# When the first four row gathers of a graph network kernel are released

## The reference

```
h    = layernorm(x)
m    = relu([h[src], edge_attr] @ W1.T + b1) @ W2.T + b2     # one message per edge
agg  = sum of the messages by destination                     # 10000 x 512
gi   = agg @ W_ih.T + b_ih ;  gh = h @ W_hh.T + b_hh
r, z = sigmoid(i_r + h_r), sigmoid(i_z + h_z) ;  n = tanh(i_n + r * h_n)
x1   = x + h + batchnorm((1 - z) * n + z * h)
out  = x1 + experts(layernorm(x1))                            # top 2 of 8, and a shared one
```

## Time and profile before

| what | value |
|---|---|
| median of three timed runs | 1315.35 us (1314.4 to 1319.97) |
| the profiled execution, its own time | 1303.76 us |
| its span, first to last instruction | 1301.9 us |
| PE busy | 1281.2 us (98% of the span) |
| DVE, POOL, ACT busy | 997.7, 816.4, 734.0 us |
| moved by the DMA engines | 179.58 MB, 138 GB/s on average |

### The profile page before, as it was taken

How to read it: one execution, slowest core, us unless ns; L and a number is a source line. 1 busy time by engine, 2 the same in 40 slices (tenths; PEclk the granted TensorE clock), 3 DMA queues, 4 the chain that set the end, 5 groups by cost and what they waited for, 6 DMA issues and landing times. The chain is left out here.

```text
span 1301.9 us, 22928 instructions
## 1 busy us (share of the span) xinstructions
PE 1281.2 (98%) x6398; PEld 1083.2 (83%) x6398; DVE 997.7 (77%) x2198; ACT 734.0 (56%) x1726; POOL 816.4 (63%) x1117
## 2 busy tenths in 40 slices
PE   8999999999899999999999999999999999999997
PEld 7788888888688888888888888888888888888885
DVE  6879575568777777777777777777777777777776
ACT  5331222134666666666666666666666666666652
POOL 3121243114777777777777777777778777777771
PEclk9999999999999999999999999999999999999999
DMA  8123554377433433333433433433433433433430
GB/s 297 43 83 135 198 198 162 125 273 240 141 132 130 135 122 129 137 121 129 137 121 129 136 121 129 136 122 129 137 121 129 137 121 129 137 121 129 136 98 33
DMA packets 64208, 179.58 MB, mean 138 GB/s; under 512 B 9456, under 2 KB 10352, under 8 KB 64048
## 3 DMA queue, kind: packets, MB, share of 16 engines
q1 hardware_dynamic: 48160, 99.20, 22.3%
q0 software_dynamic: 16016, 79.97, 18.6%
HBM read 141.86 MB, written 37.29 MB: 138 GB/s over the span
## 5 line engine op out<-in xcount | busy, mean ns | idle before, releaser
L1844 PE MATMUL bank<-whh_hi,x_hi 128*128 128x512 f32 x948 | 376.7, 397 | 2.4 <-DVE x L1774 1.6
L1844 PE MATMUL bank<-whh_hi,x_lo 128*128 128x512 f32 x948 | 370.1, 390 | 0.0
L1844 PE MATMUL bank<-whh_lo,x_hi 128*128 128x512 f32 x948 | 369.7, 390 | 0.0
L1844 PEld LDWEIGHTS bank<-whh_hi,x_hi 128*128 128x128 f32 x948 | 178.2, 188 | 38.6 <-DVE x L1774 2.0
L1844 PEld LDWEIGHTS bank<-whh_hi,x_lo 128*128 128x128 f32 x948 | 178.0, 188 | 37.8
L1844 PEld LDWEIGHTS bank<-whh_lo,x_hi 128*128 128x128 f32 x948 | 178.3, 188 | 34.3
L1593 POOL TENSOR_TENSOR h_n<-h,n_gate 128x512 f32<-128x512 f32 x78 | 101.0, 1294 | 68.7 <-ACT n_gate L1612 68.7
L1525 POOL TENSOR_TENSOR rstd<-var_eps,minus_half 128x1 f32<-128x1 f32 x158 | 90.4, 572 | 66.0 <-DVE var_eps L505 65.9
L1733 DVE TENSOR_TENSOR h_lo<-bank,h_hi 128x512 fp32r<-128x512 f32 x79 | 54.7, 692 | 77.8 <-ACT h_hi L1660 77.8
L1510 POOL DMA_INDIRECT gates<-gates_in,slot_at x78 | 83.7, 1074 | 46.7 <-issue 45.7
L1587 POOL TENSOR_TENSOR n_pre<-r_hn,gates 128x512 f32<-128x512 f32 x77 | 99.2, 1288 | 13.0 <-POOL r_hn L1583 13.0
(11 more groups left out here) (214 smaller groups left out, 3101.9 us busy)
## 6 DMA issues: line engine op xcount, KB each, us to landing
xt<-in_x SPq DMA_DIRECT2D x79, 256.0 KB, 2.8
x_lo_raw<-in_x_cols SPq DMA_DIRECT2D x79, 256.0 KB, 2.7
out<-y SPq DMA_DIRECT2D x78, 256.0 KB, 2.0
gates_in<-g_out SPq DMA_DIRECT2D x16, 768.0 KB, 3.9
whh_rows<-in_whh SPq DMA_DIRECT2D x4, 768.0 KB, 5.8
whh_lo_raw<-in_whh_t SPq DMA_DIRECT2D x4, 768.0 KB, 10.3
gates_in<-g_out SPq DMA_DIRECT2D x12, 256.0 KB, 4.3
wih_lo_raw<-in_wih_t SPq DMA_DIRECT2D x2, 1024.0 KB, 8.4
```

Of the source, the lines that this page charges most:

```text
L1844: last = pe.matmul(to[0:R, :], a[:, s, k * R:(k + 1) * R], w[:, k, q * D:(q + 1) * D], start=n == 0, stop=n == 3 * DK - 1)
```

## The change

The second of the two waits is gone. The four gathers are issued as soon as the source indices have landed. Nothing else in the kernel is different, neither the order of any engine's instructions nor any size.

```diff
             pool.iota(is_lo[:, :], pattern=[[0, 2]], base=0, channel_multiplier=1,
                       allow_small_or_imprecise_dtypes=True).then_inc(f2_step, 1)
-
             pool.wait_ge(src_in, 16)
-            pool.wait_ge(fused_in[DK - 1], 32)
             for j in range(SUP):
                 gather_source(0, j)
             pool.wait_ge(consts, 3)
```

## The result

Five timed runs of each kernel gave a median of 1314.63 us before (1313.3 to 1319.97) and 1320.89 us after (1319.4 to 1323.37). The ratio of after to before, taken over the runs of both, is 1.0042, with a 95% interval of 1.0026 to 1.0058 (the two medians alone lie 6.3 us apart). By the ratio the change costs about 5.5 us, between 3.4 and 7.6. That is clear of no change by its interval.

A forecast was written before the change was run, and what follows sets the result against it. PE, busy 98%, was taken to bound the kernel. Terms +0 (wait on POOL), +0 (earlier rows) and +2.4 us (third 1) on the 1315.35 us median gave 1317.8 us, range 1311.5 to 1323 us.

The forecast's parts named there:

- What bounds: Whole span: PE busy 98%; its 0.34 and 0.57 us waits at 37 to 39 us hang on third 1's landing.
- The gathers' start and worth: POOL's four gathers: first begins near 2.6 us, fourth near 7; earlier rows are worth nothing to their reader, DVE's statistics.
- The gathers' share: DMA queues from about 4.5 us: gathers get half the rate, all 1.05 MB through by 10.3 us, ahead of third 1.
- The delay of third 1, +2.4 us: Transfer of third 1: gathers' bytes delay it 2.7 us, less part of the free room, so 2.4 us.
- The 0.57 us stays: PE's second small wait at 37 to 39 us: unchanged at 0.57 us, being DVE's own work of two more tiles.
- The covers: PE before 37 us: later quarters and third 1 cause no wait; cover for third 1 is 4.7 us against 2.4.
- the case in which the clock falls: Rival on PE's clock: it falls, with the cases reaching up to 1322 us; chance 0.09.
- No measurable change: Total time: difference below 0.5%, 6.6 us, can't be told from no change by timing; chance of within 0.5%: 0.88.
- Nothing moves: Rival on the gathers: little rate while the direct queue is full, or wait never decided; 0 us, 1315.35 us; chance 0.15.
- DVE holds back the later gathers: Rival on POOL: DVE's splits hold it, only two gathers go ahead of third 1; +1.3 us, 1316.7 us; chance 0.11.
- Faster: Rival on PE's small waits: they go because something in DVE's chain comes sooner; -0.9 us, 1314.4 us; chance 0.05.
- SP's transfers: SP's eight transfers: issued some 6 to 8 us sooner, release between 11 and 13 us, no PE wait changed.

The follow-up runs named there:

- experiment 4: Kernel before, gathers still late, with SP issuing third 2 (1 MB) ahead of third 1; ratio to before 1.0026.
- experiment 7: Kernel after, with DVE's first two searches moved into later idle gaps, behind compare(0) and messages(1, 3); ratio to before 0.9983.
- experiment 1: Kernel before, unchanged, timed and profiled again; ratio to before 1.0003.
- experiment 8: Kernel before, with DVE's first two searches moved into later idle gaps, behind compare(0) and messages(1, 3); ratio to before 0.9973.
- experiment 10: Kernel before with the two searches in later gaps of DVE, plus 21 instead of 12 constant transposes on PE at the start; ratio to before 0.9978.
- experiment 2: Kernel after, with 28 transposes of a constant filling PE's gap at 37 to 41 us; ratio to before 1.0014.
- experiment 5: Kernel after, unchanged, timed and profiled again; ratio to before 1.0035.
- experiment 9: Kernel after, with SP's next eight transfers held back until third 2 has landed; ratio to before 1.0038.
- experiment 3: Kernel after, with DVE's two searches moved right behind the low parts of the four transposed tiles; ratio to before 1.0035.
- experiment 6: Kernel after, with the third and fourth gather again behind the last quarter, so half the bytes go early; ratio to before 1.0014.

## Why the prediction was right, and where it was not

*What bounds.* Right, but for a detail: the root at 21.00 us is not POOL's next instruction behind the gathers, it is the second of two. PE's small waits at 37 us hung on the landing of third 1 through ACT and DVE; the profile of after shows the same delay in five rows, experiment 4 makes it without any early gather, and experiment 7 takes the loss away by taking DVE's searches out of the chain.

*The gathers' start and worth.* Right: 2.82 and 6.86 us for 2.6 and near 7; no reader gained.

*The gathers' share.* Wrong. I let them take half of the rate from 4.5 us on, have all 1.05 MB through by 10.3 us, and before 12 us in any case. From 5 to 9 us they moved 0.30 MB against 1.12 MB of direct bytes, a fifth of the total, and they were through only between 13 and 13.8 us. What the term needed held all the same: third 1 landed behind all of them.

*The delay of third 1, +2.4 us.* This term was mis-sized. It measured 3.5 us against the first profile. When third 1 landed before, at 11.76 us, 3.30 MB had moved; when it landed in after, at 15.26 us, 4.54 MB had. The 1.24 MB more are the gathers' 1.05 MB and 0.19 MB of direct bytes, which I had not counted; of which transfer these are the rows don't say. At 11.76 us after had moved 3.24 MB, 0.06 MB less than before, so 1.30 MB were left, and at the 373 GB/s of the stretch from 11.76 to 15.26 us these are 3.5 us. The room for which I had taken off time was used (297 GB/s instead of 258 from 4 to 5 us, 375 instead of 289 from 11 to 12), but the rate between 5 and 11 us, 362 GB/s instead of 392, took it back. That two queues at work make the rate lower is not shown: experiment 1, with late gathers, moved 352 GB/s from 5 to 10 us, after 363 and before 388.

The first profile also had an early third 1. ACT's high part of it began at 11.84, 12.89, 13.25 and 12.06 us in the four profiles with late gathers and unchanged transfers (before, experiments 1, 8 and 10), and between 15.03 and 15.99 us in the six with all gathers early. On the same chip the distance is 2.4 to 3.0 us. So the 2.4 us is at the lower end of what the change itself does, and the rest of the 3.5 is the draw of one execution.

*"The 0.57 us stays."* Wrong, and small: at half pace the fourth tile's transposes took 1.09 us, and the third low part was ready when they were done.

*The covers.* Right: PE has no wait between 6.2 and 36.9 us, although the last quarter came to ACT at 11.95 us, 2.80 later than before. *"Third 2 lands about where it did"* was wrong by 3.6 us, without cost.

*The sum and the clock.* Here the prediction was incomplete. The likeliest case had 2.4 us and a full clock. What happened was that case together with the case in which the clock falls, to which I gave 0.09: behind the wait of 4.02 us it read 0.66 from 40 to 50 us. So the time lies in the range because the range was drawn wide enough for that case and for the scatter of the runs, and the 2.4 us of the sum are less than half of what was measured. The 1322 us at which the cases end are 1315.35 + 2.4 + 4.2. The 4.2 us for the clock was my estimate, half of the 8.5 us from PE's first work at 1.54 us to the end of its half pace at 10.0. No run shows this term: the runs showed 2.44 us in the stretch behind the wait and 2.5 us by experiment 2, on top of a delay of 3.57 us and not 2.4. The opening got longer by 6.06, and the two timed comparisons gave 5.5 and 4.6. Experiment 2 separates the two terms. No row of before showed whether a gap lowers the clock or only keeps it low. Here it lowered it: behind the waits of 3.34, 3.37, 4.02 and 4.50 us the granted clock fell (to 0.83, 0.83, 0.66 and 0.83 over the ten us), behind that of 1.48 us it did not (1.00). With the delay at 3.5 us instead of 2.4 the gap came to 4.02 us, among those behind which it fell.

Near my forecast gap of 2.7 us the traces show both outcomes, at 189 us. In experiment 5 PE was idle for 2.88 us, ran at full pace for 1.5 us, and then the clock read 0.50 from 190.8 to 194 us. In the first profile of after it was idle for 2.89 us in the same place, and the clock stayed at 1.00 until 200 us. In experiment 10 the clock fell behind gaps of 0.33, 1.00, 0.33 and 1.00 us between 181 and 185 us (0.83 from 180 to 190 us), though none of them is as long as the 1.48 us behind which it did not. So the length of one gap does not decide by itself, and at 2.7 us the clock could have gone either way.

*"No measurable change."* Wrong. I had said that a difference below 0.5% can't be told from no change by timing. The interval of five runs each reached 0.16% to either side, those of the experiments 0.09% to 0.17%, and a difference of 0.42% was clear of noise.

*The other rivals.* "Nothing moves" is out. "DVE holds back the later gathers" is out: the third and fourth gather took 0.95 us each in after, beside DVE's splits (one of 1.28 us in experiment 5), and all bytes were through before 15 us. "Faster" needed something earlier in DVE's chain, and in after nothing was; experiments 7 and 8 had to move the searches for it.

*SP's transfers.* Right by experiment 9: no cost. The estimate for SP's release, 11 to 13 us, was short of the 13.80 us measured, and SP started 5.1 us sooner and not 6 to 8, since the gathers were through later than I had them.

## What to carry to other kernels

The 1.05 MB that were issued early here were paid for by what landed behind them (third 1, 3.5 us later). So before a wait is removed one should name the first transfer that will be late and follow it to the engine that sets the end; here it was one that the diff does not mention. A wait of the bounding engine has a second price if its clock falls, here 2.4 us on top of 3.6. And a slack of a few tenths of a microsecond in one profile is less than what such a landing moves between executions, here 1.4 us with the same transfers. Where a long operation that nobody needs yet stands in the chain of a late transfer, moving it into a real gap was worth more here (ratios of 0.9983 and 0.9973 in experiments 7 and 8) than moving the transfers (1.0042), but the gap must be one whose next user is not waited for (experiment 3 against 7 and 8).

## What was not expected

*The same kernel is 8 to 10 us slower on some chips, and a part of it is visible.* Before took 1306.47, 1316.11 and 1314.27 us on the three. In the stretch in which POOL issues ten scatters of 128 single numbers each (line 744), engines of the second chip stood still, and the profile names nothing that they waited for. Longest waits from 176 to 196 us (total, times, longest), experiment 6:
```profile
ACT a_hi L848 <- remote: 16.7, 2, 14.5
...
PE bank L1327 <- issue: 6.5, 1, 6.5
DVE a_lo L1030 <- issue: 6.3, 1, 6.3
```
and on the first chip, experiment 1:
```profile
ACT a_hi L848 <- PE bank L1397: 7.7, 4, 6.6
```
where PE has no wait at all in it, nor has it in experiments 2, 3 and 4. On the third chip the waits there are shorter (1.68 and 1.00 us the longest of PE in experiments 9 and 10). "remote" and "issue" are names for a wait whose end the profile does not show. Before's first profile, 1303.76 us, has no such wait either, which fits its lying 11.6 us below the timed runs; on which chip it was taken is not known. Whether the scatters cause the waits was not tried.

*The granted clock does not show the slow start.* The first eight matmuls of the first product, from about 6 to 10 us, run at half pace in every profile here but that of experiment 10 (2.04 or 2.05 us for the first four), where only the first four do (1.91 us, then 1.07 us for the next four). Yet the granted clock of the windows reads 1.00 in before and after for both 0 to 5 and 5 to 10 us. After the wait at 40 us it does read 0.66. At the start the pace of the matmuls has to be read instead.

*SP's issues grew.* While the gathers ran, SP's issues of the last quarter, the thirds and the biases took 0.53 to 0.71 us each in after, against 0.43 to 0.51 in before. That the gathers do it is not shown: in experiment 1, without early gathers, the same issues took 0.43 to 1.24 us.
